# A two-network graph kernel: the nodes' scales made into rows by transfers, and x loaded in eight blocks

## The reference

```python
def _L0_gnn_ref(x, edge_weights, W_gcn, b_gcn, W_mlp, b_mlp, edge_index):
    ...
    A_norm = _normalized_adj(edge_index, edge_weights, N)   # dinv[:, None] * A * dinv[None, :]
    h = x
    for l in range(W_gcn.shape[0]):
        h = A_norm @ h
        h = h @ W_gcn[l] + b_gcn[l]
        h = jax.nn.leaky_relu(h @ W_mlp[l] + b_mlp[l], negative_slope=LEAKY_SLOPE)
    return h

def _gcn_conv(x, row, col, W, b, n_nodes):
    h = x @ W
    deg = jax.ops.segment_sum(jnp.ones(col.shape[0], x.dtype), col, num_segments=n_nodes)
    dis = jnp.where(deg > 0, jax.lax.rsqrt(deg), 0.0)
    norm = dis[row] * dis[col]
    msg = h[row] * norm[:, None]
    out = jax.ops.segment_sum(msg, col, num_segments=n_nodes)
    return out + b

x = _layernorm(x + _L0_gnn_ref(x, edge_weight, ...), axis=-1)
x = _layernorm(x + _L1_gnn_ref(x, edge_index, ...), axis=-1)
```

## Time and profile before

| | |
|---|---|
| median of the runs | 335.19 us (334.96 to 335.63) |
| the profiled execution | 335.47 us, its span 333.6 us |
| instructions | 4919 |
| TensorE, matmuls | 314.5 us busy, 94% |
| TensorE, weight loads | 259.7 us, 78% |
| VectorE | 189.0 us, 57% |
| ScalarE | 122.0 us, 37% |
| GpSimd (POOL) | 49.9 us, 15% |
| transfers | 13.43 MB, mean 40 GB/s |

### The profile page before, as it was taken

One profiled execution on the slowest core, in us unless ns is written; L12 is line 12 of the kernel. 1 busy time (PEld: TensorE's weight loads), 2 busy tenths in 40 slices (PEclk: granted clock), 3 DMA queues, 4 the chain that ended last, 5 costly groups with the idle time before them and its releaser, 6 DMA issues.

```text
span 333.6 us, 4919 instructions
## 1 busy us (share of the span) xinstructions
PE 314.5 (94%) x1977; PEld 259.7 (78%) x1977; DVE 189.0 (57%) x333; ACT 122.0 (37%) x253; POOL 49.9 (15%) x54
## 2 busy tenths in 40 slices
PE   2878999998999999999999999999999999999993
PEld 1767786876788888888888888888888888888882
DVE  6998999714544611165643457675953444225664
ACT  3637889546434401134432013233702444220000
POOL 2100000001005970100000011121680000001111
PEclk9999999999999999999999999999999999999998
DMA  6270000700000000000700000006100000000121
GB/s 211 66 254 2 3 2 0 249 6 2 3 0 1 2 0 0 2 0 0 238 15 0 2 0 0 0 4 226 61 2 0 0 0 2 0 4 33 63 84 73
DMA packets 8590, 13.43 MB, mean 40 GB/s; under 512 B 1906, under 2 KB 2290, under 8 KB 8564
## 3 DMA queue, kind: packets, MB, share of 16 engines
q1 hardware_dynamic: 8564, 13.05, 11.6%
HBM read 10.95 MB, written 2.10 MB: 39 GB/s over the span
## 4 chain that ended last, share of the span: by engine, by line
PE 88%; DVE 7%; issue 2%; ACT 1%; DMA 1%; POOLq 0%; POOL 0%; SPq 0%; ACTq 0%
PE psum L650 75%; PE psum L708 6%; PE psum L636 3%; DVE hot L1004 2%; PE psum L755 1%; DVE sel L996 1%; PE psum L830 1%; DVE hot L999 1%; PE psum L692 1%; DVE wm_low L1089 1%; DVE wgt_low L1076 1%; PE psum L714 1%; DMA src_i<-in_src 1%; PE psum L864 1%; ACT hot L455 0%
## 5 line engine op out<-in xcount | busy, mean ns | idle before, releaser
L441 POOL TENSOR_TENSOR small<-small 128x1 f32<-128x1 f32 x16 | 11.9, 742 | 161.6 <-DVE small L1272 161.6
L708 PE MATMUL psum<-hot,sel 128*128 128x96 bf16 x512 | 32.3, 215 | 2.1 <-DVE hot L1004 1.3
L708 PEld LDWEIGHTS psum<-hot,sel 128*128 128x128 bf16 x512 | 28.4, 101 | 7.5 <-issue 6.9
L650 PE MATMUL psum<-at_high,x_high 128*128 128x512 f32 x64 | 25.8, 403 | 0.6 <-DVE x_low L1200 0.6
L1076 DVE SCALAR_TENSOR_TENSOR y_low<-psum,small,y_high 128x512 fp32r<-128x512 f32 x16 | 11.9, 750 | 24.2 <-ACT y_high L455 24.2
L650 PE MATMUL psum<-at_low,x_high 128*128 128x512 f32 x64 | 25.1, 392 | 0.0
L650 PE MATMUL psum<-y_high,at_high 128*128 128x512 f32 x64 | 25.0, 391 | 0.0
L650 PE MATMUL psum<-cnt,x_high 128*128 128x512 f32 x64 | 25.0, 390 | 0.0
L650 PE MATMUL psum<-at_high,x_low 128*128 128x512 f32 x64 | 25.0, 390 | 0.0
L650 PE MATMUL psum<-cnt,x_low 128*128 128x512 f32 x64 | 25.0, 390 | 0.0
L650 PE MATMUL psum<-y_low,at_high 128*128 128x512 f32 x64 | 24.9, 390 | 0.0
(11 more groups left out here) (185 smaller groups left out, 755.3 us busy)
## 6 DMA issues: line engine op xcount, KB each, us to landing
wg_raw<-in_L_gnn_W_gcn SPq DMA_DIRECT2D x2, 1024.0 KB, 5.5
x_raw<-in_x SPq DMA_DIRECT2D x1, 2048.0 KB, 10.3
xs<-in_x SPq DMA_DIRECT2D x1, 2048.0 KB, 9.3
w_raw<-in_L_gnn_W SPq DMA_DIRECT2D x2, 1024.0 KB, 8.1
out<-xs SPq DMA_DIRECT2D x8, 256.0 KB, 2.0
wm_raw<-in_L_gnn_W_mlp SPq DMA_DIRECT2D x1, 1024.0 KB, 8.2
wm_next<-in_L_gnn_W_mlp SPq DMA_DIRECT2D x1, 1024.0 KB, 8.8
bias_bc<-in_L_gnn_b SPq DMA_DIRECT2D x1, 256.0 KB, 8.2
```

The costliest lines, as they stand in the source:

```text
L441: pool.tensor_tensor(r[:, 1:2], r[:, 0:1], power[:, 0:1], ALU.pow).then_inc(rstd_ready, 1)
L650: ins = pe.matmul(dest, s, m, start=first and n == 0, stop=end and n == len(pairs) - 1, skip_group_check=True)
L708: ins = pe.matmul(sums[1 if k == 0 else 0], stationary, moving, start=False, stop=False, skip_group_check=True)
```

## The change

- The matmuls of `spread` on TensorE, the ring's entries dinvb and disb, and VectorE's four copies into `col_scale` are gone. Behind them every product takes another bank: g1_b starts at bank 4 instead of 6, h2 at bank 1 instead of 3.
- SyncE has a `spread` of its own. It writes the 128x8 columns to a DRAM tensor `scales`, node by node, waits until that has landed, and loads the row of 1024 values into all partitions of `col_scale`. For dinv that is done once dinv is made (and the edge loop and `adj_ready` are over), for dis once the last h1 product has been read and dis is made.
- x comes in eight blocks of 256 KB. `X_LATE` is 2: the first two blocks lie over `bias_rows` and `last_term` and are loaded where all of x was; the other six are loaded behind the second layer's weights and bg, each after the one before has landed.
- VectorE waits for the first row before h1 and for the second before h3. ScalarE's wait for x is for all eight blocks.

```diff
@@ layout
+
+        X_LATE = -(-(cursor[B2] - B2) // (4 * D))
         again(B2)
         x_raw = at("x_raw", B2, [P, NB, D], F32)
@@
+        scales = nc.dram_tensor("scales", [2, N], F32, kind="Internal").ap()
@@ ring
-        for name, count in (("at_b", NB), ("dinvb", 2), ("g1_b", KD)):
+        for name, count in (("at_b", NB), ("g1_b", KD)):
...
-        for name, count in (("deg1", 1), ("h1", 2 * KD), ("y1", NB), ("disb", 2), ("h2", NB), ("g2", 2 * KD),
+        for name, count in (("deg1", 1), ("h1", 2 * KD), ("y1", NB), ("h2", NB), ("g2", 2 * KD),
@@ SyncE
                 sp.dma_start(bg_raw[:], bg[1].rearrange("(k p) -> p k", p=P)).then_inc(bg_in, 16)
+
+            for n, j in enumerate(range(X_LATE, NB)):
+                if n:
+                    sp.wait_ge(x_in, 16 * n)
+                sp.dma_start(x_raw[:, j, :], x[j * P:(j + 1) * P, :]).then_inc(x_in, 16)
             sp.wait_ge(done["biasb0"], 1)
             sp.dma_start(bias_rows[2:3, :], bm[1:2, :]).then_inc(bm_in, 16)
             sp.wait_ge(done["biasb1"], 1)
             sp.wait_ge(scaled, G * len(SHARED))
-            sp.dma_start(x_raw[:], x.rearrange(by_k, p=P)).then_inc(x_in, 16)
+            for j in range(X_LATE):
+                sp.dma_start(x_raw[:, j, :], x[j * P:(j + 1) * P, :]).then_inc(x_in, 16)
+
+
+            def spread(n, columns):
+                with nc.allow_non_contiguous_dma(reason="nodes' scales"):
+                    sp.dma_start(scales[n].rearrange("(b p) -> p b", p=P), columns).then_inc(scales_out, 16)
+                sp.wait_ge(scales_out, 16 * (n + 1))
+                sp.dma_start(col_scale[:], scales[n:n + 1, :].broadcast_to([P, N])).then_inc(scales_in, 16)
+
+            sp.wait_ge(loop_done, 1)
+            sp.wait_ge(adj_ready, 1)
+            sp.wait_ge(dinv_ready, 1)
+            spread(0, dinv)
             sp.wait_ge(done["h1"], 2 * KD)
             sp.dma_start(xs[:], x.rearrange(by_k, p=P)).then_inc(x_again_in, 16)
+            sp.wait_ge(taken["h1"], 2 * KD)
+            sp.wait_ge(pow_ready, 2)
+            spread(1, dis)
             sp.wait_ge(done["h2"], NB)
@@ ScalarE
-                    act.wait_ge(x_in, 16)
+                    act.wait_ge(x_in, 16 * NB)
@@ TensorE, ahead of g1_b
-            pe.wait_ge(dinv_ready, 1)
-            for h in range(2):
-                spread("dinvb", h, dinv)
@@ TensorE, ahead of h2
-            pe.wait_ge(pow_ready, 2)
-            for h in range(2):
-                spread("disb", h, dis)
@@ VectorE
-            for h in range(2):
-                dve.wait_ge(done["dinvb"], h + 1)
-                if h == 0:
-                    dve.wait_ge(loop_done, 1)
-                dve.tensor_copy(col_scale[:, h * BANK:(h + 1) * BANK], bank("dinvb", h)).then_inc(taken["dinvb"], 1)
...
-            dve.wait_ge(taken["dinvb"], 2)
+            dve.wait_ge(scales_in, 16)
...
-            for h in range(2):
-                dve.wait_ge(done["disb"], h + 1)
-                dve.tensor_copy(col_scale[:, h * BANK:(h + 1) * BANK], bank("disb", h)).then_inc(taken["disb"], 1)
-            dve.wait_ge(taken["disb"], 2)
...
+            dve.wait_ge(scales_in, 32)
             for n in range(2 * KD):
                 scale_row("h3", n)
```

More of the change, by code:

```diff
@@ L318, in gnn_resnorm @@
         gen_turned = sem("gen_turned")
+        scales_out, scales_in = sem("scales_out"), sem("scales_in")
         deg_ready, pow_ready, dinv_ready = sem("deg_ready"), sem("pow_ready"), sem("dinv_ready")
@@ L322, in gnn_resnorm @@
         stages = ("wgt0", "wgt1", "wc0", "wc1", "at", "at_b", "g1_a", "g1_b", "y1", "g2", "y3")
-        plain = ("bias0", "bias1", "biasb0", "biasb1", "dinvb", "deg1", "disb", "h1", "h2", "h3", "h4")
+        plain = ("bias0", "bias1", "biasb0", "biasb1", "deg1", "h1", "h2", "h3", "h4")
         done = {s: sem(f"{s}_done") for s in stages + plain}
@@ L824, in at_parts @@
                 return at_high[:, s, c], at_low[:, s, c]
[L826 to L832, removed]
             for j in range(3):
```

## The result

The changed kernel takes 331.38 us (median of four runs, 331.32 to 331.40), the kernel before beside it 335.25 us. The ratio is 0.9888, with a 95% interval from 0.9874 to 0.9903: faster by 1.1%, or 3.9 us. The profiled execution took 331.32 us, its span is 329.5 us.

What follows compares the result with a forecast made beforehand. TensorE, busy without a gap from 110 to 320 us, was taken as the bound. Profiled 335.47 us less 3.57 us for the spreading matmuls, other terms 0, gave 331.90 us; the median, 0.28 us lower, 331.6 us, range 330.6 to 332.8 us.

Steps and rivals of the forecast that it cites:

- The term of the sum: TensorE's queue: removing the spreading matmuls saves their spacing in the chain, 3.57 us, bounds 3.4 to 3.9 us.
- the two places: Spreading matmuls before g1_b (112.16 us) and before h2 (181.11 us): 16 rows each, worth 1.79 and 1.78 us.
- The next work starts earlier: g1_b and h2 on TensorE: operands ready with margins of 3.2 and 3.3 us, so each 1.8 us saving passes through.
- the 0.7 us that the prediction allowed: Stretch before 110 us: a change there of more than 0.7 us would count as the prediction being wrong.
- x is worth nothing: x in eight loads: it already had 13.8 us of cover before ScalarE's first reading, so the term is 0.
- rival that x disturbs TensorE: Gaps at 66.75 and 71.08 us go with the 2 MB x load: another 0.63 us off, 331.0 us; chance 0.12.
- SyncE's queue: Early x blocks ahead of the second bias row's load: fifth block in at 35.9 us, no delay, term 0.
- The slower rival: Early x blocks hold SyncE, delaying the bias row: 339.5 us at 8.2 us per block, deciding from 6.2; chance 0.05.
- The scale transfers: Scale rows through DRAM: complete between 85 and 113 us and between 175 and 203 us, hidden before their readers, term 0.
- Two savings of one price: Before g1_b and before h2 on TensorE: each saving of 1.8 us passes through alike, 3.57 us together.

Runs made afterwards that it cites:

- e1: The changed kernel with x put back to one load at its old place, scale rows still by transfers: 331.42 us, ratio 0.9893 to the kernel before.
- e4: The changed kernel with all eight x blocks loaded at the old place near 58 us, without waits: 331.38 us.
- e10: The changed kernel with each of the first five early x blocks loaded twice, one load after the other: 331.33 us, ratio 0.9895 to the kernel before.
- e3: The kernel before with each spreading matmul issued twice, 32 more rows in the trace: 338.57 us, ratio 1.0111 to the kernel before.
- e2: The kernel before with x in eight blocks as in the change, scales still spread by TensorE: 334.89 us, ratio 0.9996 to the kernel before.
- e7: The changed kernel with each of the first five early x blocks loaded three times, one after the other: 345.70 us, ratio 1.0319 to the kernel before.
- e11: The changed kernel with scales written to DRAM in SBUF order, 32 bytes per partition, so permuted: 331.30 us, ratio 0.9896 to the kernel before.
- e9: The changed kernel with the second scale set (dis) again spread by TensorE and copied by VectorE: 334.08 us, ratio 0.9973 to the kernel before.
- e8: The changed kernel with the eight degree matmuls behind g1_b in the one-pass fast float32 format: 330.47 us, ratio 0.9867 to the kernel before.
- e6: The changed kernel with one more write of 128x8 single values to DRAM near 59 us: 331.48 us, ratio 0.9886 to the kernel before.

## Why the prediction was right

**The term of the sum.** 3.57 us from the chain at the two places. The one execution pair differs by 335.47 - 331.32 = 4.15 us, the medians of the first comparison by 3.87 us, and the three variants that keep only the scale transfers' part or all of it (e1, e4, e10) lie 3.51, 3.55 and 3.60 us below the kernel before beside them. e3 adds 3.64 us by doubling. These four medians stand within 0.1 us of the term; the interval of one such ratio is 0.5 us to either side. That the forecast of 331.6 us came within 0.2 us is partly luck: it went from 335.19 us, and the kernel before had medians from 334.93 to 335.25 us. The additional 0.58 us of the profiled pair, 4.15 - 3.57, is nearly all in the two stops of the earlier trace rows: 0.39 us, and 0.24 us where e1, e3 and the changed kernel have 0.08 us.

**The next work starts earlier.** Right: no wait of TensorE between 110 and 320 us, g1_b behind the turns at 111.55 us. That is 0.6 us before the 112.16 us at which it could have begun, just inside the 0.7 us that the prediction allowed for the part before 110 us; the 0.6 us are again mostly those of the two stops.

**x is worth nothing.** Right (e2, e4). The rival that x disturbs TensorE, 0.12, is wrong as a cause of the median; I had taken a stop in one execution as the kernel's property.

**SyncE's queue.** I expected the fifth block in at 35.9 us; the sixth is issued by 37.2 us, directly behind the fifth's landing: 1 us later than worked out, because the blocks follow each other at 2.65 us and not at 2.4 us. The Trainium skill's fit for transfers issued by GpSimd (DMA: Bandwidth & Descriptors, section Anatomy of one DMA) gives, by estimate, 2.6 us for a block. The trace agrees for SyncE's blocks: 2.6 us. The slower rival has the right place, and its threshold of 6.2 us per block lies between e10 (two loads of 2.65 us for each of the five, nothing lost) and e7 (three loads, 8 us). Its way of pricing was too cheap: applied to e7 it gave 12 us, and 14.3 us were lost, because it leaves out the clock.

**The scale transfers.** Hidden, as predicted, the first row at 95.2 us lies inside the bounds of 85 to 113 us, the second at 177.4 us inside those of 175 to 203 us. The Trainium skill's rule is that a strided last dimension becomes one descriptor per element (same page, Rules for kernel authors). The trace agrees: 1040 packets under 512 bytes for the first write, and e11 takes 1.4 us against 9.5 us. One thing was missing in this step: I let the second write wait behind the xs load and did not ask what it does to xs. xs lands 16.4 us after its issue in place of 9.3 us, which leaves 12 us of cover of what would have been 19 us.

**Two savings of one price.** The prediction treats the two places alike. In the chain they are; in the time, e9 shows that having only the first one costs 0.9 us more than its rows. So my sum lacked a term: what a shift of TensorE's program can cost elsewhere, perhaps by its instruction loads. In the changed kernel it happens to be nothing, which is luck; nothing in the prediction could have told so.

## What to carry to other kernels

Where one engine is busy without a gap for 200 us, a small instruction of its queue is worth its spacing, whether it is a helper that makes rows or a degree sum: price it in the chain, not by busy time, and move it to an engine or a queue that idles. Check then that the substitute is issued early enough: here a pair of transfers of 15 us is free when it is complete 43 us ahead of its reader, and turns the gain into a loss when it is issued behind g1_b. And compare more than one execution before a stop that one profile shows is given a cause.

## What the runs showed of the hardware that I had not expected

- A 4 KB write to DRAM as 1024 single values took 9.5 us in the changed kernel, and 12.9 us beside the xs load; in 128 short rows (e11) it took 1.4 and 5.5 us. An instruction load of 16 KB beside the first write took 3.9 us, against 1.1 us in the kernel before. The 2 MB load of xs beside the second write took 15.4 to 17.0 us in four profiles (the changed kernel, e1, e4, e8) and 11.8 us in e10, but 9.2 us in e6 and e7, like the 9.0 to 9.7 us of the kernels without such a write; so it can be slowed, and is not always.
- A stop of TensorE of 11.5 us was followed by 12 us of full work at a mean granted clock of 0.70, and one of 3.4 us in two pieces by 4 us at 0.57. By the profiles that costs 3.6 and 1.7 us beyond the stops' own length.
- Sixteen matmul rows, at their proper price of 1.78 us, came with a stop of about 1.3 us 45 us further on, behind a branch; with the transfers idle it stayed, and with other numbers of rows it was not there.
